# Reordering the stretch ahead of the loop in a modulated-attention and fusion-MLP kernel

## The chip, the cores and the metric

The kernel runs on one core of a Trainium2 chip. The metric is the device time of one execution in microseconds (us), median of the runs shown. The core's engines are TensorE (PE, matmuls), VectorE (DVE), ScalarE (ACT), GpSimd (POOL) and SyncE (SP, here only a queue of DMA issues). Each runs its own list of instructions strictly in order, and they meet only at semaphores.

## The reference

The input `x` is 4 x 1024 x 512, with conditioning vectors of 256, 64 and 32 numbers for each of the 4 batches. Two parts follow one another; both add their result to their input:

```
kx  = x @ (w * style * demod) + b              # modulated linear, weights differ by batch
A   = softmax(kx_heads @ kx_heads.T / sqrt(32)) # over the 16 heads of one token
x   = x + modulated_linear(A @ kx_heads)
h   = LN(LN(x, pw[id], pw_b[id]), cp[id], cp_b[id]);  t = LN(x, tm..);  s = LN(x, ms..)
m, n, r = x + LN(silu(cond @ W1 + b1) @ W2 + b2)     # for the three conditioning vectors
x   = x + LN(silu(concat(w0 h, w1 t, w2 m, w3 n, w4 r, w5 s) @ int_W1 + b) @ int_W2 + b)
```

The tables for gains and biases are small (5, 5 and 3 rows), so the kernel multiplies them by the parts of `int_W1` once, ahead of the loop, and adds the right row by a matmul with one-hot ids. The parts of `int_W1` for m, n and r act on the same `x`, so they are summed once into one weight (`x` below).

## The kernel before

The 4096 tokens are 32 tiles of 128. The loop runs k = 1 to 16. Pass k does the attention ("front") of tiles a = 2k and b = 2k+1 and the fusion MLP ("back") of tiles pa = 2k-2 and pb = 2k-1 side by side. Fp32 accuracy is got from products of a high and a low part (`three` on TensorE), so every operand and every weight is split: ACT rounds the high part, DVE or POOL subtracts for the low one.

Ahead of the loop stands a long straight stretch, about 88 us, in which the weights are loaded, modulated and split, the tables are made, and tiles 0, 1 and 2 go through parts of the attention. Its order is written out by hand on each engine. There is no planner. The names that matter:

- TensorE: `tables_tsh` multiplies the bias tables of t, s and h by `raw_t`, `raw_s`, `raw_h` (12 matmuls of 512 columns, three at a time on separate 32-column parts of the array). `tables_mnr` does the same with the rows of m, n, r, which ACT writes to `L` (L1013) from the transposed vectors of `vec_T`. `scores(g)` and `values(g)` are the two attention products of tile g in the PSUM tile `att`; `out_proj(g)` and `proj(g)` are the two modulated linears; `a_T`, `z_T`, `x_T`, `u_T` are transposes. `mlp1` and `mlp2` are the conditioning MLPs.
- ScalarE: `q_hi(g)` (L816) rounds the result of `proj(g)`; `e_first(g)` (L856) rounds the transposed softmax of tile g into `e`, `gain_tables` makes `Gt`, `Gs`, `Gh`, `split_hi` rounds a weight, `z_make` (L878) applies the first layer norm, `value_low` (L846) copies half of `values`.
- VectorE: `e_T` (L1329 to L1335) is the softmax's sum, division and transpose; `e_second` (L1339) the low part of `e`, on which `values` waits. `vectors_norm` and `vectors_end` (L1251, L1256, L1258) finish the m, n, r vectors in `p_h`, on which `vec_T` waits. `x_one` (L1358 to L1364) adds the residual and takes statistics; `q_lo` (L1290), `q_T` (L1297); `a_sum` (L1345, L1347); `x_weights` (L1284) sums the m, n, r weights into `stg_e`, 8 pieces in all; `x_low` (L1274) makes the low part of that sum, 4 pieces; `x1_lo(g)` (L1376) is the low part of the tile's x, which also frees the PSUM bank that `x_T(1)` waits for.
- GpSimd: no order changes there. It scales the scores, roots the variances, gathers pathway rows by DMA, and makes low parts of the weights t, s, h.
- SyncE: `blocks_q(g)` and `blocks_v(g)` copy transposed tiles into the block-diagonal tile `BD`, 4 DMAs each; `blocks_q(1)` waits for the end of `values(0)`.

Of the kernel before, what the change touches and what calls it, by code (L numbers as in the profile page):

```python
# [75 lines left out]
def build(nc, A, out):  # L76
    ctx = ExitStack()
    with ctx:
        s = {n: ctx.enter_context(nc.semaphore("s_" + n)) for n in SEMS}
# [321 lines left out]
        def _(e):  # L401
# [74 lines left out]
            def vec_T():  # L476
                e.wait_ge(s["h2"], 6)
                o = bank(("vT", 0))
                for c in range(4):
                    i = e.transpose(o[:, c * 128:c * 128 + 128], h2[:, c * 128:c * 128 + 128], ident[:, :])  # L480
                i.then_inc(s["vTr"], 1)

            def tables_tsh():

                e.wait_ge(s["LB"], 3)
                for n in "tsh":
                    e.wait_ge(s["c_r" + n], 16)
                for kt in range(4):
                    for n, quarter in (("t", 0), ("s", 1), ("h", 3)):
                        i = mm(Pp[quad(quarter), :], L[n][:, kt, :], raw[n][:, kt, :], start=(kt == 0))  # L490
                        if kt == 3:
                            i.then_inc(s["Pm"], 1)
# [13 lines left out]
            def proj(g, kts=range(4)):  # L506

                o = tok[1 if g else 0]
                on_bias = g > 3 and g % 2 == 0
                if kts[0] == 0:  # L510
                    if g == 0:
                        e.wait_ge(s["c_one"], 48)
                        e.wait_ge(s["tq"], 1)
                    elif on_bias:
                        e.wait_ge(s["sd"], g // 2 - 1)
                    elif g == 2:
                        e.wait_ge(s["ql"], 2)
                    elif g > 3:
                        e.wait_ge(s["wc"], g // 2 - 1)
                    elif g == 3:  # L520
                        e.wait_ge(s["ql"], 3)
                    e.wait_ge(s["xlo"], g + 1)
                for kt in kts:
                    if g % 8 == 0:
                        e.wait_ge(s["mwl"], 8 * (g // 8) + kt + 1)
                    i = three(o[:, :], xhi[:, kt, :], xlo[:, kt, :], WL["k", "h"][:, kt, :], WL["k", "l"][:, kt, :], kt == 0 and not on_bias)
                if kts[-1] == 3:
                    if not on_bias:
                        i = mm(o[:, :], selT[:, :].to_broadcast([128, 128]), tab[:, :])
                    i.then_inc(s["A"], 1)  # L530

            def scores(g):
                if g:
                    e.wait_ge(s["AVs"], 2 * g)
                e.wait_ge(s["bq"], 64 * (g + 1))
                for j in range(16):
                    both = att[:, j * 64:j * 64 + 64].rearrange("p (m t) -> p m t", t=2)
                    q = q12[:, j // 2, :, j % 2, :]
                    mm(both, diag(j, 0), q, start=(j % 8 == 0))
                    i = mm(both[:, :, 0], diag(j, 1), q[:, :, 0])  # L540
                    if j % 8 == 7:
                        i.then_inc(s["S"], 1)

            def values(g):
                e.wait_ge(s["bv"], 64 * (g + 1))
                e.wait_ge(s["e2"], g + 1)
                for j in range(16):
                    c = slice(j * 32, j * 32 + 32)
                    both = att[:, j * 64:j * 64 + 64]
                    mm(both, diag(j, 0), e12[:, c, :].rearrange("p m t -> p (m t)"), start=(j % 8 == 0))  # L550
                    i = mm(both.rearrange("p (m t) -> p m t", t=2)[:, :, 0], diag(j, 1), e12[:, c, 0])
                    if j % 8 == 7:
                        i.then_inc(s["AV"], 1)
# [23 lines left out]
            def out_proj(g):  # L577
                o = att if g == NG - 1 else tok[0]
                if g == NG - 1:
                    e.wait_ge(s["AVs"], 2 * g + 2)  # L580
                elif g % 2 == 0 and g:
                    e.wait_ge(s["x1"], g)
                elif g > 2:
                    e.wait_ge(s["w"], g - 2)
                elif g == 1:
                    e.wait_ge(s["x1"], 1)
                else:
                    e.wait_ge(s["ql"], 1)
                e.wait_ge(s["alo"], g + 1)
                for kt in range(4):  # L590
                    if g % 8 == 0:
                        e.wait_ge(s["mwl"], 8 * (g // 8) + 4 + kt + 1)
                    i = three(o[:, 0:512], ahi[:, kt, :], alo[:, kt, :], WL["o", "h"][:, kt, :], WL["o", "l"][:, kt, :], kt == 0)
                i.then_inc(s["O"], 1)
# [63 lines left out]
            proj(1)  # L658
            mod_rows(1)
            mlp1()  # L660
            tables_tsh()
            values(0)
            demod_T()
            mlp2()
            a_T(0)
            scores(1)
            out_proj(0)
            proj(2)
            vec_T()
            tables_mnr()  # L670
            values(1)
            z_T(0)
            a_T(1)
            scores(2)
# [81 lines left out]
        def _(e):  # L756
# [54 lines left out]
            def q_hi(g):  # L811
                e.wait_ge(s["A"], g + 1)
                e.wait_ge(s["sc"], 2 * g + 2)
                if g:
                    e.wait_ge(s["qT"], g)
                e.activation(qt[:, :, 0], tok[1 if g else 0][:, :], ACT.Copy, scale=inverse(g)).then_inc(s["qh"], 1)  # L816
# [35 lines left out]
            def e_first(g):  # L852
                e.wait_ge(s["ET"], 2 * g + 2)
                if g:
                    e.wait_ge(s["AV"], 2 * g)
                e.copy(e12[:, :, 0], att[:, 512:1024]).then_inc(s["e1"], 1)  # L856
# [88 lines left out]
            def gain_tables():  # L945

                e.wait_ge(s["tq"], 1)
                for i, n in enumerate("tsh"):
                    e.activation(GT[n][:, :], tab[:, :], ACT.Copy, scale=cst[:, 5 + i:6 + i]).then_inc(s["G"], 1)

            def split_hi(dst, src, sem):
                for kt in range(4):
                    i = e.copy(dst[:, kt, :], src[:, kt, :])
                i.then_inc(sem, 1)
# [53 lines left out]
            x_scaled()  # L1008
            exponential(1)
            gain_tables()  # L1010
            e.wait_ge(s["vTr"], 1)
            for i, n in enumerate("mnr"):
                j = e.activation(L[n][:, :, 0:24].rearrange("p k (r c) -> p k r c", c=8)[:, :, :, 0:4],  # L1013
                                 four(xp[XP["vT", 0][0]])[:, :, 32 * i:32 * i + 4].unsqueeze(2).to_broadcast([128, 4, 3, 4]), ACT.Copy, scale=w7[:, 2 + i:3 + i])
                j.then_inc(s["LB"], 1)
            q_hi(2)
            e_first(1)
            e.wait_ge(s["m2"], 3)
            e.wait_ge(s["c_rt"], 16)
            split_hi(W1["t", "h"], raw["t"], s["wh"])  # L1020
            z_make(0)
            value_low(1)
            e.wait_ge(s["Pm"], 15)
# [122 lines left out]
        def _(e):  # L1146
# [100 lines left out]
            def vectors_norm():  # L1247
                r = slice(0, 96)
                mv = small[r, 72:74]
                e.wait_ge(s["lnB"], 2)  # L1250
                e.tensor_scalar(h2[r, :], h2[r, :], mv[:, 0:1], small[r, 75:76], ALU.subtract, ALU.mult).then_inc(s["h2"], 1)  # L1251

            def vectors_end():
                r = slice(0, 96)
                e.wait_ge(s["h2"], 4)
                e.tensor_tensor(h2[r, :], h2[r, :], rv[1][r, :], ALU.mult).then_inc(s["h2"], 1)  # L1256
                e.wait_ge(s["h2"], 5)
                e.tensor_tensor(h2[r, :], h2[r, :], rv[2][r, :], ALU.add).then_inc(s["h2"], 1)  # L1258
# [19 lines left out]
            def x_weights(n, kts):  # L1278

                src, land = ((stg["a"], "c_rn"), (raw["r"], "c_rr"))[n - 1]  # L1280
                e.wait_ge(s[land], 16)
                e.wait_ge(s["xc"], n)
                for kt in kts:
                    i = e.scalar_tensor_tensor(out=stg["e"][:, kt, :], in0=src[:, kt, :], scalar=w7[:, 2 + n:3 + n], in1=stg["e"][:, kt, :], op0=ALU.mult, op1=ALU.add)  # L1284
                    if n == 2 or kt == 3:
                        i.then_inc(s["xc"], 1)
# [50 lines left out]
            def e_second(g):  # L1337
                e.wait_ge(s["e1"], g + 1)
                e.tensor_tensor(e12[:, :, 1], att[:, 512:1024], e12[:, :, 0], ALU.subtract).then_inc(s["e2"], 1)  # L1339
# [123 lines left out]
            score_sum(1)  # L1463
            less_max(1)
            vectors_norm()
            vectors_end()
            x_weights(1, (0,))
            e_T(1)
            x_one(0)
            e_second(1)  # L1470
            q_lo(2)
            q_T(2)
            a_sum(1)
            x_weights(1, (1, 2))
            a_lo(1)
            x_weights(1, (3,))
            v_stats(0)
# [4 lines left out]
            score_sum(2)  # L1482
            x_low((0,))
            x_one(1)
            x_low((1,))
            x1_lo(0)
            x_low((2, 3))
            e.wait_ge(s["Pm"], 16)
            e.wait_ge(s["c_rp"], 32)
            e.tensor_tensor(rp[:, :], rp[:, :], Pp[:, :], ALU.add).then_inc(s["pa"], 1)  # L1490
# [433 lines left out]
```

## Time and profile before

| | us |
|---|---|
| median of three runs | 871.07 |
| lowest, highest | 868.79, 872.23 |
| span of the profiled execution, first to last instruction | 867.6 |
| PE busy | 836.8 (96%) |
| DVE, POOL, ACT busy | 646.7, 605.7, 487.6 |
| mean granted TensorE clock | 0.989 of full |

The profile has the span of the profiled execution and no further time of its own for it; the median of the runs lies 3.5 us above the span. Busy shares are means over all stages: PE is nearly always busy from 92 us on, and has its gaps ahead of that.

### The profile page before, as it was taken

Reading aid. Unit: us, or ns where it says so; the run is one execution under the profiler, and the core shown is the slowest. Engines: PE = TensorE matmul, PEld = TensorE weight load, DVE = VectorE, ACT = ScalarE, POOL = GpSimd, SP = SyncE. Lnnn points to the kernel's source line nnn. Section 1 sums busy time; section 2 is a strip of 40 time slices with the busy share of each in tenths; the row PEclk is TensorE's granted clock in tenths of the full one; section 3 lists DMA queues with packets and bytes.
Section 4 is the critical chain, followed back from the end, with each engine's and each line's share of the span. In section 5 each row is a group of like instructions: output and inputs, shape, how many; then the busy total and the mean of one; then the engine's idle time right before and its main releaser. Section 6 shows DMA issues by size and latency. Waiting matters only on the chain.

```text
span 867.6 us, 19685 instructions
## 1 busy us (share of the span) xinstructions
PE 836.8 (96%) x7456; PEld 731.9 (84%) x7474; DVE 646.7 (75%) x1067; ACT 487.6 (56%) x851; POOL 605.7 (70%) x766
## 2 busy tenths in 40 slices
PE   5996999999999999999999999999999999999997
PEld 5853888988889898888989898888988898898986
DVE  3589778778786867678797877679797767677652
ACT  3567555565656465465656556465647546464531
POOL 2367998778786767768776866668787775756472
PEclk9998999999999999999999999999999999999999
DMA  8972233424343333525243332424343342323110
GB/s 277 419 268 62 71 91 105 126 63 150 83 151 81 98 93 86 128 51 158 71 149 89 107 93 69 127 68 145 83 123 91 87 117 49 104 68 83 47 50 25
DMA packets 104365, 95.55 MB, mean 110 GB/s; under 512 B 72880, under 2 KB 78160, under 8 KB 102608
## 3 DMA queue, kind: packets, MB, share of 16 engines
q1 hardware_dynamic: 95056, 69.26, 27.7%
q0 software_dynamic: 4608, 16.78, 7.1%
q10 hardware_dynamic: 4608, 8.25, 2.8%
q8 instruction: 60, 0.98, 0.5%
q14 instruction: 33, 0.27, 0.1%
HBM read 69.60 MB, written 8.40 MB: 90 GB/s over the span
## 4 chain that ended last, share of the span: by engine, by line
PE 88%; DVE 5%; DMA 2%; POOL 2%; issue 1%; ACT 1%; ACTq 0%; another core or an unknown queue 0%; DVEq 0%; POOLq 0%
PE acc L405 43%; PE tok L405 28%; PE att L405 8%; PE xp L558 6%; PE xp L405 3%; DMA kb<-in_kb 1%; DVE stg_e L1284 1%; DMA pgb<-in_pw,pidx 1%; DVE raw_k L1170 0%; DVE W1xl L1274 0%; POOL op0l L1706 0%; DVE qt L1290 0%; POOL W2l L1710 0%; DVE q L1297 0%; DVE BD L1185 0%
## 5 line engine op out<-in xcount | busy, mean ns | idle before, releaser
L1706 POOL TENSOR_TENSOR op1l<-ytmp,op1h 128x512 fp32r<-128x512 f32 x64 | 89.8, 1403 | 20.1 <-ACT op1h L912 19.6
L1652 POOL TENSOR_TENSOR xlo<-xraw,xhi 128x512 fp32r<-128x512 f32 x31 | 40.5, 1306 | 68.0 <-ACT xhi L804 68.0
L405 PE MATMUL acc<-op0h,W1xh 128*128 128x256 f32 x256 | 75.8, 296 | 1.4 <-DVE op0l L1376 1.1
L405 PE MATMUL acc<-op1h,W1th 128*128 128x256 f32 x256 | 75.0, 293 | 0.0
L405 PE MATMUL acc<-op1h,W1hh 128*128 128x256 f32 x256 | 73.7, 288 | 0.0
L405 PE MATMUL acc<-op0h,W1sh 128*128 128x256 f32 x256 | 73.7, 288 | 0.0
L405 PE MATMUL acc<-op1h,W1tl 128*128 128x256 f32 x256 | 72.4, 283 | 0.0
L405 PE MATMUL acc<-op1l,W1hh 128*128 128x256 f32 x256 | 72.4, 283 | 0.0
L405 PE MATMUL acc<-op1l,W1th 128*128 128x256 f32 x256 | 72.4, 283 | 0.0
L405 PE MATMUL acc<-op0h,W1sl 128*128 128x256 f32 x256 | 72.4, 283 | 0.0
L405 PE MATMUL acc<-op1h,W1hl 128*128 128x256 f32 x256 | 72.4, 283 | 0.0
L405 PE MATMUL acc<-op0l,W1sh 128*128 128x256 f32 x256 | 72.4, 283 | 0.0
L405 PE MATMUL acc<-op0l,W1xh 128*128 128x256 f32 x256 | 72.3, 282 | 0.0
L405 PE MATMUL acc<-op0h,W1xl 128*128 128x256 f32 x256 | 72.3, 282 | 0.0
L912 ACT CAST op1h<-ytmp 128x512 fp32r<-128x512 f32 x64 | 39.6, 619 | 46.9 <-DVE ytmp L1390 44.8
L1691 POOL TENSOR_TENSOR pgb<-z,pgb 128x512 f32<-128x512 f32 x32 | 48.0, 1499 | 15.1 <-DMA pgb<-in_pw,pidx 14.1
L1670 POOL TENSOR_TENSOR SE<-SE,wT 128x512 f32<-128x512 f32 x32 | 34.1, 1066 | 33.9 <-DVE SE L1324 33.6
L1390 DVE TENSOR_TENSOR ytmp<-zT,xp 128x512 f32<-128x512 f32 x64 | 43.6, 682 | 17.9 <-ACT zT L892 12.9
L405 PE MATMUL tok<-Wkh,xhi 128*128 128x512 f32 x128 | 56.0, 438 | 0.2
L405 PE MATMUL tok<-W2h,op0h 128*128 128x512 f32 x128 | 52.8, 412 | 0.0
L405 PE MATMUL tok<-Wkl,xhi 128*128 128x512 f32 x128 | 51.4, 402 | 0.0
L405 PE MATMUL tok<-Wkh,xlo 128*128 128x512 f32 x128 | 51.3, 401 | 0.0
(269 smaller groups left out, 3005.2 us busy)
## 6 DMA issues: line engine op xcount, KB each, us to landing
xsq<-in_x SPq DMA_DIRECT2D x32, 256.0 KB, 3.1
xb<-in_x SPq DMA_DIRECT2D x32, 256.0 KB, 3.0
out<-xb SPq DMA_DIRECT2D x32, 256.0 KB, 2.4
BD<-q SPq DMA_DIRECT2D x124, 64.0 KB, 2.1
BD<-v SPq DMA_DIRECT2D x124, 64.0 KB
xraw<-in_xT SPq DMA_DIRECT2D x30, 256.0 KB, 3.0
ring<-in_k_wT ACTq DMA_DIRECT2D x6, 256.0 KB, 3.3
dmb<-dm_rows SPq DMA_DIRECT2D x6, 256.0 KB, 3.9
```

The source lines that it names most:

```text
L405: return e.matmul(o, a, b, start=start, stop=True, skip_group_check=True)
L558: i = e.transpose(o[:, c * 128:c * 128 + 128], src[:, c * 128:c * 128 + 128], ident[:, :])
L912: e.copy(op[slot]["h"][:, :, half(g)], four(ytmp[YT[n, g][0]])).then_inc(s[f"o{n}h"], 1)
L1284: i = e.scalar_tensor_tensor(out=stg["e"][:, kt, :], in0=src[:, kt, :], scalar=w7[:, 2 + n:3 + n], in1=stg["e"][:, kt, :], op0=ALU.mult, o ...
L1390: e.tensor_tensor(four(y), src, four(xp[XP[n, g][0]]), ALU.mult).then_inc(s["p" + n], 1)
L1652: e.tensor_tensor(xlo[:, :, :], (xraw1 if g == 1 else xraw)[:, :, :], xhi[:, :, :].bitcast(F32), ALU.subtract).then_inc(s["xlo"], 1)
L1670: e.tensor_tensor(c, c, wT[g % 2][:, :].unsqueeze(2).to_broadcast([128, 32, 16]), ALU.mult).then_inc(s["wS"], 1)
L1691: e.tensor_tensor(pg, z[:, :], pg, ALU.mult).then_inc(s["v"], 1)
L1706: e.tensor_tensor(op[slot]["l"][:, :, half(g)], four(ytmp[YT[n, g][0]]), op[slot]["h"][:, :, half(g)].bitcast(F32), ALU.subtract).then_inc ...
```

## The change

Only the order of calls changes, on three engines; no instruction is added or removed.

- TensorE: `tables_tsh` moves from ahead of `values(0)` to behind `scores(1)`; `values(1)` moves from behind `tables_mnr` to ahead of `vec_T`.
- ScalarE: the three copies into `L` for m, n, r, with their wait for `vec_T`, move behind `q_hi(2)`, `e_first(1)` and the rounding of the t weights.
- VectorE: `e_T(1)` and `e_second(1)` move ahead of `vectors_end` and of `x_one(0)`; the first piece of `x_weights(1)` joins the second and third, behind `a_sum(1)`; `x1_lo(0)` moves ahead of the second piece of `x_low`.

```diff
 (TensorE)
             mlp1()
-            tables_tsh()
             values(0)
             demod_T()
             mlp2()
             a_T(0)
             scores(1)
+            tables_tsh()
             out_proj(0)
             proj(2)
+            values(1)
             vec_T()
             tables_mnr()
-            values(1)
             z_T(0)
 (ScalarE)
             exponential(1)
             gain_tables()
+            q_hi(2)
+            e_first(1)
+            e.wait_ge(s["m2"], 3)
+            e.wait_ge(s["c_rt"], 16)
+            split_hi(W1["t", "h"], raw["t"], s["wh"])
             e.wait_ge(s["vTr"], 1)
             for i, n in enumerate("mnr"):
...
-            q_hi(2)
-            e_first(1)
-            e.wait_ge(s["m2"], 3)
-            e.wait_ge(s["c_rt"], 16)
-            split_hi(W1["t", "h"], raw["t"], s["wh"])
             z_make(0)
 (VectorE)
             vectors_norm()
+            e_T(1)
+            e_second(1)
             vectors_end()
-            x_weights(1, (0,))
-            e_T(1)
             x_one(0)
-            e_second(1)
             q_lo(2)
             q_T(2)
             a_sum(1)
-            x_weights(1, (1, 2))
+            x_weights(1, (0, 1, 2))
...
             x_low((0,))
             x_one(1)
-            x_low((1,))
             x1_lo(0)
-            x_low((2, 3))
+            x_low((1, 2, 3))
```

## Rows read from the trace of the kernel before

**Rows 1.** The page: span, and busy time of each engine.
```profile
span 867.6 us, 19685 instructions
...
PE 836.8 (96%) x7456; PEld 731.9 (84%) x7474; DVE 646.7 (75%) x1067; ACT 487.6 (56%) x851; POOL 605.7 (70%) x766
```

**Rows 2.** PE's waits, 88 to 160 us: total, times, longest.
```profile
PE xp L558 <- DVE op0l L1376: 2.9, 1, 2.9
PE xp L558 <- ACT pgb L883: 1.3, 1, 1.3
```

**Rows 3.** Windows: length, each engine's busy time, clock, DMA share, GB/s.
```profile
90.00:120.00 30.00, 30.00 (x276) 27.21 (x276) 24.44 (x38) 17.29 (x32) 28.56 (x30) 0.99 0.36 85
```

**Rows 4.** Timeline of PE, 45 to 89 us: start, duration, operation, idle before.
```profile
45.80 0.62 PE L405 MATMUL acc<-raw_t,Lt 128*32 128x512 f32 x1
...
51.06 1.25 PE L405 MATMUL att<-e,BD 128*128 128x64 f16 x32
...
52.46 0.62 PE L405 MATMUL acc<-stg_b,p_hT 128*32 128x512 f32 x1
...
56.02 0.66 PE L558 MATMUL xp<-ident,ET 128*128 128x128 f32 x4
56.72 1.23 PE L405 MATMUL att<-q,BD 128*128 128x64 f16 x32
58.51 0.38 PE L405 MATMUL tok<-Woh,ahi 128*128 128x512 f16 x1 [0.55 <-issue]
...
60.90 0.58 PE L405 MATMUL tok<-Wkh,xhi 128*128 128x512 f32 x1
...
63.64 0.39 PE L405 MATMUL tok<-Wkh,xlo 128*128 128x512 f32 x1
...
88.04 1.09 PE L558 MATMUL xp<-ident,xb 128*128 128x128 f32 x4 [2.86 <-DVE op0l L1376]
```

**Rows 5.** Windows of 1 us; the clock is the third number from the end.
```profile
47.00:48.00 1.00, 1.00 (x9) 0.33 (x6) 1.00 (x2) 0.98 (x2) 0.00 (x0) 0.50 1.05 432
...
50.00:51.00 1.00, 1.00 (x9) 0.12 (x3) 1.00 (x2) 1.00 (x3) 0.63 (x1) 1.00 0.26 86
```

**Rows 6.** Timeline of DVE, 47 to 87 us.
```profile
47.75 0.73 DVE L1339 TENSOR_TENSOR e<-att,e 128x512 f16<-128x512 f32 x1
...
53.88 1.06 DVE L1347 STREAM_TRANSPOSE ET<-SE 128x512 f32<-128x512 f32 x1
...
61.50 1.43 DVE L1256 TENSOR_TENSOR p_h<-p_h,p_rv 96x512 f32<-96x512 f32 x1
62.96 1.67 DVE L1258 TENSOR_TENSOR p_h<-p_h,p_rv 96x512 f32<-96x512 f32 x1
64.55 0.74 DVE L1284 SCALAR_TENSOR_TENSOR stg_e<-stg_a,w,stg_e 128x512 f32<-128x512 f32 x1
...
66.94 0.73 DVE L1335 STREAM_TRANSPOSE att<-SE 128x512 f32<-128x512 f32 x1
...
71.71 0.76 DVE L1345 TENSOR_TENSOR SE<-att,SE 128x256 f32<-128x256 f32 x2
72.50 1.05 DVE L1347 STREAM_TRANSPOSE ET<-SE 128x512 f32<-128x512 f32 x1
73.47 2.87 DVE L1284 SCALAR_TENSOR_TENSOR stg_e<-stg_a,w,stg_e 128x512 f32<-128x512 f32 x2
...
85.91 1.39 DVE L1274 SCALAR_TENSOR_TENSOR W1xl<-stg_e,W1xh 128x512 fp32r<-128x512 f32 x1
```

**Rows 7.** Timeline of ACT, 62 to 72 us.
```profile
62.58 0.60 ACT L850 ACTIVATE att<-SE 128x512 f32<-128x512 f32 x1
...
65.94 0.86 ACT L816 ACTIVATE qt<-tok,tok_s 128x512 f16<-128x512 f32 x1
...
67.70 0.75 ACT L856 CAST e<-att 128x512 f16<-128x512 f32 x1 [0.90 <-DVE att L1335]
...
70.60 0.82 ACT L878 ACTIVATE z<-xb,nm,small 128x512 f32<-128x512 f32 x1
```

## The prediction

> **What bounds the kernel now.** I read the page first. PE is busy 836.8 of 867.6 us [rows 1], so a change of order can only move PE's 31 idle us, or change the clock that its matmuls get. Then I read PE's waits and the windows. Behind 88 us there are two waits worth a name up to 160 us, 2.9 us of `x_T(1)` on the low part of tile 0's x and 1.3 us of `u_T(2)` on ACT [rows 2], and 90 to 120 us is 30.00 busy of 30 [rows 3]. So the loop is bound by PE, and whatever the change does must show as a shift of the moment at which PE reaches those two places. The reader is to see in [rows 3] also that POOL is busy 28.56 of the same 30 us: POOL has hardly any room to catch up if it enters the loop late.
>
> Ahead of the loop I followed the chain of waits and then each engine's timeline. From scores(1) at 56.72 [rows 4] the chain leaves PE and runs almost wholly over DVE until the 2.9 us wait ends at 88.04 [rows 4]. In DVE's timeline the rows of that stretch stand nearly back to back, as the four from 61.50 on do [rows 6]. It is bound by DVE in its order, and PE's matmuls there lie beside it.
>
> **The change part by part.** I carry one number along: how much later (+) or earlier (-) each engine is than before.
>
> *values(0) without the tables ahead.* Before, tables_tsh ran from 45.80 to 51.06 and values(0) behind it [rows 4]. Its operand was ready at 48.48 [rows 6], so now it starts there, 2.6 us sooner, with PE idle between. demod_T and mlp2 follow at once. mlp2 took 3.56 us (52.46 to 56.02) [rows 4]. At full clock it would end near 53.6, but a_T(0) behind it needs the transpose that ends at 54.94 [rows 6]; that wait doesn't move, because it hangs on ACT's rounding of the o weights. So the gain for a_T(0) is at most 1.1 us. The clock decides what of it comes: before, at 47 us it was 0.50, the 1.2 GHz level, though PE was busy in the whole of that stretch, and 1.00 again at 50 us with the tables still running [rows 5]. Now there is a gap where those tables were, so I let half speed last into mlp2, until about 53 us. Then values(0) takes some 1.9 us instead of 1.25, and mlp2 ends at about 55.6. I take -0.4 us for a_T(0), scores(1) and the softmax chain behind them; the bounds are 0 and -1.1.
>
> The Trainium skill (TensorE: Matmul & The Clock Gate, Part 1) says that the throttled state is the default and that activity releases it. The trace agrees so far that the clock returned during the tables [rows 5]. By that rule the gap ahead of values(0) postpones the return, and the gain would be near -0.4 rather than the -1.1 of the full clock.
>
> *The tables behind scores(1).* scores(1) now ends near 57.55 (57.95 less 0.4). The tables are 12 matmuls of the same shape as mlp2's, so at full clock 3.5 us by mlp2 [rows 4] (at the mixed clock of before, 5.3). They cover 0.55 us that PE waited ahead of out_proj(0), and delay it by the rest. out_proj(0) took 2.39 us and proj(2) 3.13 (60.90 to the end of the row at 63.64) [rows 4]. So proj(2) ends at 57.55 + 3.5 + 2.4 + 3.1 = 66.55 instead of 64.03: +2.5 us. The bounds are 65.9 (early softmax) and 68.3 (5.3 us of tables).
>
> *Who is queued behind it.* On ACT, q_hi(2) waits for proj(2), and e_first(1) stands behind q_hi(2) in both orders. Before, q_hi(2) ran at 65.94 and cost nobody anything, since e_first(1) waited until 67.66 for DVE's transpose [rows 6, 7]. Now DVE does e_T(1) straight behind vectors_norm. The exponential, which ended at 63.18 [rows 7], ends near 62.75, and e_T(1) takes 2.4 us (as before: from the end of the row at 64.55 to 67.67, the end of the one at 66.94 [rows 6]), so the transpose is ready at 65.2. But ACT stands at q_hi(2) until 66.55. Its rounding and e_first(1), 0.8 and 0.75 us [rows 7], end at 68.1. e_second(1), next on DVE, waits from 65.2 to 68.1. That is 2.9 us of idle DVE with vectors_end, x_one(0), q_lo(2), q_T(2) and everything after it queued behind. There is another 1.7 us idle ahead of e_T(1) (from 61.1, where vectors_norm now ends, to 62.75), where vectors_end ran before.
>
> *vectors_end.* Its two additions took 1.43 and 1.67 us [rows 6], with POOL busy all the while. A comparable DVE instruction beside an idle POOL took 0.74 [rows 6]. At 68.7 us POOL is waiting for x_one(0), so I give both together 1.4 us instead of 3.1. This is the one thing the new order makes cheaper on DVE.
>
> *DVE's sum.* e_second, x_one, q_lo and q_T took the 4.05 us from 67.67 to 71.71 [rows 6]. Now they and vectors_end take 5.45, from 68.1: 73.6, that is +1.9. a_sum(1) is later still, because ACT reaches value_low(1) only behind z_make(0), which started 3.0 us after x_one(0) did (67.6 to 70.60) [rows 6, 7]. x_one(0) now starts at 70.1, z at 73.1, and half a copy later a_sum(1) starts at about 74.2: +2.5. Ahead of a_lo(1) stands one more piece of x_weights. Alone it took 0.74 us; two of them beside POOL took 2.87 [rows 6]. I take 1.2, between 0.7 and 1.4, nearer the latter since POOL does tile 0's affine and the low part of x(3) then. So DVE is +3.7 us from there on, through x_weights(2), x_one(1) and x_low. POOL follows (its root of tile 0 waits for DVE's v_stats, and the low parts of the t weights stand behind it): +3.6.
>
> *x_low.* Taking x1_lo(0) ahead of one piece of x_low saves 1.39 us [rows 6] for x_T(1), not for DVE as a whole. So x_T(1) is +3.7 - 1.4 = +2.3, and with it proj(3) and the first W1 matmuls. The weights' low part and the last sum ahead of them are also due 2.2 to 2.3 us after where W1 started, so they don't hold it longer.
>
> *tables_mnr.* It ran in a gap at 65.8. Now it waits for vectors_end (70.1), vec_T and ACT's copies, and runs from about 71 to 74, with z_T(0) due at 73.9 behind it: hidden. If it ran longer, a_T(1) at 76.1 is the next with work of weight, so up to 2 us more are covered. The same holds for values(1), at 68.8 instead of 70.0, and for the DMAs of blocks_q(1), which go out 2 us sooner; scores(1) waits for a_T(0) anyway.
>
> *In the loop.* PE arrives +2.3, DVE and POOL +3.6. PE's next wait is u_T(2), 1.3 us in [rows 2], at the end of a chain over POOL's gather of tile 2 and the affine behind it. POOL has only 1.4 idle us in the 30 up to 120 us [rows 3], and what it waited for there comes later now too. So it stays about +3.3 us there and PE's wait grows by 1. Behind that PE has nothing to win back. The sum is +3.3 us: 870.9 on the profiled span of 867.6. The median of the runs is 3.5 above the span, so 871.1 + 3.3 = 874.4.
>
> The Trainium skill (SBUF — State Buffer, SBUF: two separate sides) says that DVE instructions with two SBUF inputs and GpSimd instructions lock one shared pair of ports against each other, one waiting for the whole of the other. The trace agrees: 2.87 us for two of such pieces beside POOL against 0.74 for one alone [rows 6]. By the rule the moved x_weights piece would cost a whole POOL instruction more and DVE would be +3.9.
>
> **The rivals.**
> 1. *DVE's chain isn't held (the other side of the sign).* Place: e_second(1). If proj(2) ended by 64.4, ACT would be through in time and the 2.9 us of idle go. With the earliest start (-0.7 more) and the cheap x_weights piece (-0.5) the sum is 3.3 - 2.9 - 0.7 - 0.5 = -0.8: 870.3. For it speaks that this is where vectors_end gets cheaper; against it that out_proj and proj alone need 5.5 us and the tables 3.5. Even so it is not 0.5% faster; that would need the clock to stay high at 88 us as well. Chance 0.08, with 0.04 for faster by over 0.5%.
> 2. *It does nothing that the time shows.* Idle DVE is filled back by shorter waits on POOL, and the later wait of u_T doesn't grow: 3.3 less 1.0 (u_T) less 1.3 of port waits gives about +1: 872.1. Chance 0.19. For it: port waits are some 3.7 us of DVE's stretch by [rows 6] alone (3.1 for 1.4, 2.9 for 1.5, 1.4 for 0.7) and shift freely.
> 3. *The clock.* Place: tables_tsh, out_proj(0), proj(2). If the low level of [rows 5] comes with them, the tables take up to 7 us and what follows up to 3 more, all ahead of q_hi(2). It decides as soon as proj(2) ends behind 68.5; each us there is a us of DVE's idle. Two to three us more give +6: 877. Against it: by the trace the clock was full from 50 us on. Chance 0.16.
> 4. The forecast, +1.5 to +5, has 0.57.
>
> **How the numbers follow.** A measurement of this kernel tells about 0.5% (4.35 us) from no change, so the bounds are 866.7 and 875.4. Of the forecast's 0.57 some three quarters lie within; with rivals 1 and 2 that makes 0.66 for same. Slower gets the last quarter and nearly all of the clock rival: 0.30. Faster: 0.04. The range, 870.3 to 878.0, goes from rival 1's time to a little above rival 3's.
>
> **What would show it.** Right: PE idle ahead of values(0) for about 2.7 us; out_proj(0) starting near 61; a DVE wait of 2 to 3 us on ACT's e ahead of L1339; L1256 and L1258 near 0.7 us each; x_T(1) at about 90.3; the wait of u_T(2) over 2 us. Wrong: no DVE wait ahead of L1339, or x_T(1) ahead of 88; a clock of 0.5 between 57 and 66 us; or POOL catching up by 120 us.

## The result, and the profile after

The changed kernel took 873.97 us (median of 8 runs, 872.34 to 874.92) against 870.03 us (median of 8, 868.79 to 872.23) for the kernel before. The ratio is 1.0043, with a 95% interval of 1.0031 to 1.0055: slower by 3.9 us by the medians and 3.7 by the ratio, where 3.3 were forecast. The loss is clear of zero, and its middle value lies below the half per cent that was called no change.

The page of the changed kernel, span and busy times:

```profile
span 872.7 us, 19702 instructions
...
PE 840.6 (96%) x7474; PEld 733.7 (84%) x7474; DVE 644.6 (74%) x1067; ACT 488.0 (56%) x851; POOL 604.9 (69%) x766
```

The span is 5.1 us longer than in [rows 1], but not all of that is the change's. Here is DVE's timeline of the changed kernel, from e_second(0) on, the point at which the orders of the two kernels part:

```profile
49.23 0.72 DVE L1339 TENSOR_TENSOR e<-att,e 128x512 f16<-128x512 f32 x1
...
61.78 0.53 DVE L1251 TENSOR_SCALAR p_h<-p_h,small 96x512 f32<-96x512 f32 x1
64.07 0.69 DVE L1329 TENSOR_REDUCE small<-att 128x16 f32<-128x512 f32 x1 [1.75 <-ACT att L850]
...
69.50 0.73 DVE L1339 TENSOR_TENSOR e<-att,e 128x512 f16<-128x512 f32 x1 [2.96 <-ACT e L856]
70.12 0.67 DVE L1256 TENSOR_TENSOR p_h<-p_h,p_rv 96x512 f32<-96x512 f32 x1
70.83 0.69 DVE L1258 TENSOR_TENSOR p_h<-p_h,p_rv 96x512 f32<-96x512 f32 x1
...
75.61 0.76 DVE L1345 TENSOR_TENSOR SE<-att,SE 128x256 f32<-128x256 f32 x2 [0.69 <-ACT SE L846]
...
77.39 3.55 DVE L1284 SCALAR_TENSOR_TENSOR stg_e<-stg_a,w,stg_e 128x512 f32<-128x512 f32 x3
...
81.47 1.84 DVE L1284 SCALAR_TENSOR_TENSOR stg_e<-stg_a,w,stg_e 128x512 f32<-128x512 f32 x1
```

e_second(0) starts at 49.23, where it was 47.75 [rows 6]. Nothing ahead of it was changed. In this execution DVE waited 1.36 us instead of 0.45 for the load of `pidx` near 19 us, and the lag grew to 1.48 by here. So I take 1.48 us off the changed kernel's times before comparing, and give places as times since the start of e_second(0). By that the span grew by 3.6 us, close to the 3.9 of the medians. The reader is to see the two new waits, 1.75 us ahead of the softmax's sum and 2.96 us ahead of `e`, and vectors_end at 0.67 and 0.69 us instead of 1.43 and 1.67 [rows 6].

The second of these waits is for ACT, and ACT itself waited for PE. In ACT's timeline `q_hi(2)` (L816) is held by `proj(2)`, and `e_first(1)` (L856) comes only behind it:

```profile
68.07 0.83 ACT L816 ACTIVATE qt<-tok,tok_s 128x512 f16<-128x512 f32 x1 [2.17 <-PE tok L405]
68.76 0.71 ACT L856 CAST e<-att 128x512 f16<-128x512 f32 x1
```

PE's timeline of the changed kernel, with the places that [rows 4] has:

```profile
50.10 1.87 PE L405 MATMUL att<-e,BD 128*128 128x64 f16 x32 [2.73 <-DVE e L1339]
...
52.33 1.06 PE L405 MATMUL acc<-stg_b,p_hT 128*32 128x512 f32 x1
...
57.09 0.66 PE L558 MATMUL xp<-ident,ET 128*128 128x128 f32 x4
57.59 1.22 PE L405 MATMUL att<-q,BD 128*128 128x64 f16 x32
58.73 0.62 PE L405 MATMUL acc<-raw_t,Lt 128*32 128x512 f32 x1
...
62.30 0.39 PE L405 MATMUL tok<-Woh,ahi 128*128 128x512 f16 x1
...
92.22 0.98 PE L558 MATMUL xp<-ident,xb 128*128 128x128 f32 x4 [2.82 <-DVE op0l L1376]
...
96.40 0.47 PE L405 MATMUL acc<-op0h,W1xh 128*128 128x256 f32 x1
```

The gap ahead of values(0) is 2.73 us. values(0) takes 1.87 us and mlp2's first matmuls 1.06 instead of 0.62. The windows show the clock (third number from the end) at the 1.2 GHz level there, and at full speed only behind 54.8 us:

```profile
51.00:52.00 1.00, 1.00 (x21) 0.90 (x18) 1.00 (x3) 1.00 (x3) 0.00 (x0) 0.50 0.22 68
...
54.00:55.00 1.00, 1.00 (x9) 0.31 (x6) 0.97 (x3) 1.00 (x4) 1.00 (x2) 0.60 0.50 108
```

PE's waits from 88 to 160 us in the changed kernel are the two of [rows 2], hardly changed:

```profile
PE xp L558 <- DVE op0l L1376: 2.8, 1, 2.8
PE xp L558 <- ACT pgb L883: 1.4, 1, 1.4
```

So the loss isn't a longer wait at these two places. PE and DVE come to x_T(1) later together.

### The profile page after: what moved, and what is told of

It is laid out like the page before. It is cut to its first block, busy times and chain, and to the rows that moved or that the text cites. A ratio compares the mean times of both kernels' runs of the same rounds, so it can differ in the third digit from the quotient of the medians.

```text
span 872.7 us, 19702 instructions
## 1 busy us (share of the span) xinstructions
PE 840.6 (96%) x7474; PEld 733.7 (84%) x7474; DVE 644.6 (74%) x1067; ACT 488.0 (56%) x851; POOL 604.9 (69%) x766
## 4 chain that ended last, share of the span: by engine, by line
PE 86%; POOL 4%; DVE 3%; DMA 2%; issue 1%; ACT 1%; ACTq 0%; SPq 0%; POOLq 0%; DVEq 0%
PE acc L405 42%; PE tok L405 28%; PE att L405 8%; PE xp L558 6%; PE xp L405 3%; DMA kb<-in_kb 2%; DMA pgb<-in_pw,pidx 1%; POOL W1tl L1708 1%; POOL W1sl L1708 1%; DVE stg_e L1284 0%; POOL small L1596 0%; ACT BD L934 0%; SPq L303 0%; POOL pgb L1691 0%; POOL pgb L1689 0%
```

## The experiments

Each experiment was timed against the kernel before on the same chip, 5 to 12 runs each. The places below are us since the start of e_second(0), each from that kernel's profiled execution: the start of a_T(0); DVE's wait ahead of e_second(1); the starts of x_T(1), of the first W1 matmul, and of u_T(2). Behind u_T(2) the code of all kernels is the same, and this last stretch still took between 738.4 and 740.9 us. So the ratio is the verdict, and the places, each from a single execution, tell where it comes from; the two agree within about 1.7 us. W1 stands for the first W1 matmul.

| kernel | a_T(0) | wait | x_T(1) | W1 | u_T(2) | ratio to before |
|---|---|---|---|---|---|---|
| before | 8.27 | 0 | 40.29 | 44.16 | 81.28 | 1 |
| changed | 7.86 | 2.96 | 42.99 | 47.17 | 84.30 | 1.0043 [1.0031, 1.0055] |
| e1 tables home | 8.40 | 0.79 | 41.54 | 46.36 | 84.00 | 1.0019 [1.0007, 1.0031] |
| e2 e_first ahead | 8.07 | 0.80 | 41.01 | 44.15 | 82.52 | 1.0017 [1.0008, 1.0025] |
| e3 vectors early | 8.03 | 1.67 | 41.81 | 46.63 | 83.43 | 1.0021 [1.0009, 1.0033] |
| e4 x_low old | 8.21 | 2.96 | 44.63 | 49.44 | 87.11 | 1.0048 [1.0033, 1.0062] |
| e5 x_low only | 8.18 | 0 | 39.34 | 42.34 | 80.12 | 0.9994 [0.9982, 1.0006] |
| e6 tables only | 7.84 | 0.49 | 40.62 | 43.21 | 80.81 | 1.0009 [0.9998, 1.0020] |
| e7 tables behind proj | 8.16 | 0.81 | 41.08 | 44.23 | 82.62 | 1.0023 [1.0013, 1.0033] |
| e8 fill, clock | 7.88 | 2.96 | 42.99 | 46.17 | 84.00 | 1.0041 [1.0028, 1.0055] |
| e9 piece in gap | 8.33 | 0.80 | 39.73 | 42.86 | 81.61 | 0.9994 [0.9984, 1.0004] |
| e10 split tables, x_low | 7.15 | 0 | 37.65 | 40.79 | 78.83 | 0.9972 [0.9961, 0.9983] |
| e11 split tables | 7.49 | 0 | 39.31 | 43.14 | 80.14 | 0.9990 [0.9980, 1.0000] |
| e12 split and fill | 7.40 | 0 | 39.77 | 42.34 | 79.80 | 0.9978 [0.9969, 0.9987] |

**e1: the tables home again.** On TensorE, in the changed kernel:

```diff
             mlp1()
+            tables_tsh()
             values(0)
...
             scores(1)
-            tables_tsh()
             out_proj(0)
```

> The changed kernel with tables_tsh put back ahead of values(0); all else as changed. Forecast's theory (DVE is held by ACT's wait for proj(2) behind the tables): no gap ahead of values(0), proj(2) ends 2.5 us sooner than in the changed kernel, measured from e_second(0), the DVE wait ahead of e_second(1) falls from 2.96 us to below 0.8, and the time comes to +0.6 to +1.5 us over the kernel before (about 871.3; ratio 1.001 to 1.002). Rival (DVE's own new order, above all the x_weights piece, makes the loss): the wait falls, but the time stays within 1 us of the changed kernel's 873.97.

Measured 872.63 us, 1.0019 to before: 1.7 us over it by the ratio and 1.9 by the medians, a little more than the 0.6 to 1.5 that I expected. The wait fell to 0.79 us as forecast, and the time fell with it, by 0.0024 of the 0.0043. The rival, that DVE's own order makes the loss, has the rest of it: 0.0019 is left with the tables where they were. x_T(1) came 1.45 us sooner than in the changed kernel, W1 only 0.81. Between the two the granted clock was lower: 0.50 in e1 (89.34 to 94.16 us) against 0.59 in the changed kernel (92.22 to 96.40). At u_T(2) only 0.30 us were left in e1's profiled execution, less than its time gained.

**e2: e_first(1) ahead of q_hi(2).** On ACT, the tables left where the change put them:

```diff
-            q_hi(2)
             e_first(1)
+            q_hi(2)
```

> The changed kernel with e_first(1) ahead of q_hi(2) on ACT, so that nothing on ACT's way to e_second(1) waits for proj(2); the tables stay behind scores(1). Forecast's theory: the DVE wait ahead of e_second(1) falls from 2.96 to about 0.8 us (ACT's own 0.75), everything behind it comes 2.1 us sooner, and the time is 1.7 to 2.2 us below the changed kernel (ratio to before 1.002, about 871.9). Rival (the tables cost through out_proj(0) and proj(2) themselves, as PE work in the way): less than 0.7 us below the changed kernel.

Measured 872.45 us, 1.0017. DVE's waits from 60 to 72 us in e2:

```profile
DVE small L1329 <- ACT att L850: 1.8, 1, 1.8
DVE e L1339 <- ACT e L856: 0.8, 1, 0.8
```

Two lines exchanged on ACT give as much as the tables' return. So what this part of the loss hangs on isn't the tables' 3.5 us on PE, but that ACT stands at q_hi(2) with e_first(1) behind it. x_T(1) came 1.98 us sooner, as expected (2.1). W1 stands at 44.15, where it stood before the change, and yet the kernel is 1.5 us slower than before: u_T(2) is 1.24 us later. Between W1 and u_T(2) PE now waits 0.49 us for DVE's `e` and 0.30 for POOL's low part, which it doesn't in the kernel before. This is the lag of DVE and POOL that the prediction placed in the loop.

**e3: vectors_end ahead of e_T(1).** On DVE:

```diff
             vectors_norm()
+            vectors_end()
             e_T(1)
             e_second(1)
-            vectors_end()
```

> The changed kernel with vectors_end put back ahead of e_T(1) on DVE, in the 1.75 us in which DVE waits for the exponential. The two additions should take about 3 us again beside POOL (0.67 and 0.69 in the changed kernel), e_T(1) starts about 1.4 us later, and that is hidden behind the wait for q_hi(2), which shrinks to about 1.5 us; x_one(0) comes 1.3 us sooner and tables_mnr leaves the stretch behind values(1). Forecast's theory: 1.0 to 1.4 us below the changed kernel (about 872.7, ratio to before 1.003). Rival (a DVE idle time that is only refilled by slower instructions): no gain, within 0.4 us of the changed kernel.

Measured 873.07 us, 1.0021: below the changed kernel by about 1.9 us by the ratios and 0.9 by the medians, where 1.0 to 1.4 were expected (the intervals of the ratios just overlap). x_T(1) came 1.18 us sooner, u_T(2) 0.87. The timeline of e3:

```profile
62.07 1.43 DVE L1256 TENSOR_TENSOR p_h<-p_h,p_rv 96x512 f32<-96x512 f32 x1
63.53 1.64 DVE L1258 TENSOR_TENSOR p_h<-p_h,p_rv 96x512 f32<-96x512 f32 x1
65.10 0.68 DVE L1329 TENSOR_REDUCE small<-att 128x16 f32<-128x512 f32 x1
...
69.22 0.73 DVE L1339 TENSOR_TENSOR e<-att,e 128x512 f16<-128x512 f32 x1 [1.67 <-ACT e L856]
```

The same two instructions, a multiplication and an addition, take 3.07 us beside POOL and 1.36 without it. Dear as they are there, most of it lies in time that was lost anyway: the wait ahead of e_second(1) is 1.67 us instead of 2.96.

**e4: x_low in its old order.**

```diff
             x_one(1)
+            x_low((1,))
             x1_lo(0)
-            x_low((1, 2, 3))
+            x_low((2, 3))
```

> The changed kernel with x_low in its old order (second piece ahead of x1_lo(0)). If PE's entry into the loop sets the end (as the trace of the changed kernel has it: PE and POOL both 4.5 us later at values(2)), x_T(1) comes 0.7 to 1.4 us later and the time is 0.7 to 1.4 us above the changed kernel (about 875.1, ratio to before 1.006). Rival (POOL's and DVE's lag set the end through u_T(2), as the prediction had it): x_T(1) is later, but u_T(2) waits that much less, and the time is within 0.4 us of the changed kernel.

Measured 875.57 us, 1.0048. Against the changed kernel that is 0.4 us by the ratios and 1.6 by the medians, with intervals that overlap, so the time alone decides between neither theory. The places speak against the rival: x_T(1) is 1.64 us later, W1 2.27 and u_T(2) 2.81, and PE's wait at u_T(2) is no shorter (1.37 us against 1.39). By the places the reorder of x_low is the part of the change that helps. The times of e4, e5 and of e10 against e11 all point the same way, each by less than its intervals can tell.

**e5: the kernel before with that reorder alone.**

```diff
-            x_low((1,))
             x1_lo(0)
-            x_low((2, 3))
+            x_low((1, 2, 3))
```

> The kernel before with one part of the change alone: x1_lo(0) ahead of the second piece of x_low. Forecast's theory: x_T(1) comes 1.4 us sooner; W1 starts up to 1.4 us sooner, since the last sum and x1_lo(1) on DVE end 1.4 us ahead of where W1 started; behind it DVE and POOL have gained nothing, so part of it is given back at u_T(2). Time 0.3 to 1.4 us below before (ratio 0.9985 to 0.9997). Rival (POOL's chain to u_T(2) decides alone): W1 starts sooner, but the time is within 0.3 us of before.

Measured 869.82 us, 0.9994: 0.5 us or 1.0 below before by ratio and median, and not told from it. x_T(1) came 0.95 us sooner, not 1.4, since DVE now waited 0.38 us for ACT ahead of x1_lo(0). W1 came 1.82 us sooner: the clock from x_T(1) to W1 was 1.00 instead of 0.64, and the stretch took 3.00 us instead of 3.87. At u_T(2) 1.16 us were left.

**e6: the kernel before with the tables moved alone.**

```diff
             mlp1()
-            tables_tsh()
             values(0)
...
             scores(1)
+            tables_tsh()
             out_proj(0)
```

> The kernel before with one part alone: tables_tsh behind scores(1); the orders of ACT and DVE and of values(1) as before. Forecast's theory: the same delay of proj(2) (2.1 to 2.5 us), but now x_one(0) stands ahead of e_second(1) on DVE and hides a part; ACT's vec_T wait, q_hi(2) and e_first(1) come later, the DVE wait ahead of e_second(1) is about 1 us, a_sum(1) about 1.5 us later. Time 1.0 to 1.8 us above before (ratio 1.0012 to 1.002). Rival (the new DVE order alone makes the loss): within 0.5 us of before.

Measured 871.27 us, 1.0009 (0.9998 to 1.0020), below the 1.0012 that I expected at least; the interval holds it, and no loss as well. DVE in e6:

```profile
68.32 0.18 DVE L1364 BATCH_NORM_AGGREGATE small<-small 128x2 f32<-128x6 f32 x1
68.99 0.77 DVE L1339 TENSOR_TENSOR e<-att,e 128x512 f16<-128x512 f32 x1 [0.49 <-ACT e L856]
...
71.99 0.76 DVE L1345 TENSOR_TENSOR SE<-att,SE 128x256 f32<-128x256 f32 x2 [0.36 <-ACT SE L846]
```

The wait is 0.49 us, since x_one(0) still stands ahead of e_second(1). a_sum(1) is 0.33 us later than before, not 1.5. So the move of the tables alone costs at most 1.7 us and perhaps nothing; with DVE's new order it costs the 2.96 us wait. By the ratios the tables alone cost 0.8 us (e6), the new orders without them 1.7 (e1), both together 3.7. That the whole is more than the parts is shown by the waits (0.49, 0.79 and 2.96 us), and only suggested by the times.

**e7: the tables behind proj(2).** In the changed kernel:

```diff
             scores(1)
-            tables_tsh()
             out_proj(0)
             proj(2)
+            tables_tsh()
             values(1)
```

> The changed kernel with tables_tsh behind proj(2) instead of ahead of out_proj(0): the same matmuls, on TensorE between scores(1) and values(1) in both. Forecast's theory (what counts is that they stand ahead of proj(2), on which ACT waits): the DVE wait ahead of e_second(1) falls from 2.96 to about 0.8 us, the time to that of the kernel with e_first(1) ahead, 1.5 to 2.2 us below the changed kernel (ratio to before about 1.002). Rival (the gap and the low clock ahead of mlp2 cost, wherever the tables go): within 0.7 us of the changed kernel.

Measured 872.20 us, 1.0023, and the places are those of e2 within 0.1 us. That shows it from the other side: the same matmuls between scores(1) and values(1), with the same gap ahead of values(0), cost some 1.7 us less once proj(2) doesn't wait for them.

**e8: the clock at x_T(1).** In the changed kernel 12 matmuls into a free bank, whose result nobody reads, are added ahead of `x_T(1)`:

```diff
+                if k == 1:
+                    for _ in range(12):
+                        mm(mlp[:, :], xhi[:, 0, :], WL["k", "h"][:, 0, :], True)
                 if front:
                     x_T(pb)
```

> The changed kernel plus 12 matmuls of 128x512 into a free PSUM bank, whose result nobody reads, between the first quarter of proj(3) and x_T(1), where PE waits 2.8 us and the granted clock falls to 0.5. Clock theory: they last about 2.8 us in the wait, the clock stays at 1.0, and x_T(1) to the first W1 matmul takes 3.1 to 3.3 us instead of 4.18, so the time falls by 0.7 to 1.0 us (ratio to before about 1.0033). Rival (what the clock gives back is only waited for later, on DVE's x1_lo(1) and in the loop): W1 starts sooner, the time stays within 0.3 us. If the 12 run at 1.2 GHz they take 5 us and x_T(1) is up to 2 us later: slower.

Measured 873.59 us, 1.0041. PE in e8:

```profile
87.93 2.91 PE L405 MATMUL acc<-Wkh,xhi 128*128 128x512 f32 x12
90.90 0.63 PE L558 MATMUL xp<-ident,xb 128*128 128x128 f32 x4
...
94.08 0.36 PE L405 MATMUL acc<-op0h,W1xh 128*128 128x256 f32 x1 [0.25 <-DVE op0l L1379]
```

The clock stayed at 1.00, and x_T(1) to W1 took 3.18 us instead of 4.18. Of the 1.00 us that this gave, 0.30 were left at u_T(2), and 0.2 us in the time by the ratios. PE waited 0.25 us for DVE ahead of W1, 0.47 ahead of values(2), and 0.3 for POOL, none of which it did in the changed kernel. The rival fits: at this place most of what a faster PE gains is waited for later. The time alone, with intervals of 1.2 us to either side, doesn't separate the two theories; the places do.

**e9: the x_weights piece in the gap.** e2, and on DVE:

```diff
             vectors_norm()
+            x_weights(1, (0,))
             e_T(1)
...
             a_sum(1)
-            x_weights(1, (0, 1, 2))
+            x_weights(1, (1, 2))
```

> The changed kernel with e_first(1) ahead of q_hi(2), and the first piece of x_weights(1) taken back behind vectors_norm, into the 1.75 us in which DVE waits for the exponential. Forecast's theory (the moved piece costs DVE 1.2 us or more where the change put it, POOL being busy there): a_lo(1) and x_low come 0.7 to 1.2 us sooner than with e_first(1) ahead alone, and the time is 0.5 to 1.0 us below that kernel's (ratio to before 1.0006 to 1.0012). Rival: the piece is free where it is, time as there (ratio 1.0017).

Measured 870.31 us, 0.9994: 2.0 us below e2 by the ratios, where 0.5 to 1.0 were expected. DVE in e9:

```profile
62.29 1.55 DVE L1284 SCALAR_TENSOR_TENSOR stg_e<-stg_a,w,stg_e 128x512 f32<-128x512 f32 x1
64.12 0.69 DVE L1329 TENSOR_REDUCE small<-att 128x16 f32<-128x512 f32 x1 [0.29 <-ACT att L850]
...
75.28 2.90 DVE L1284 SCALAR_TENSOR_TENSOR stg_e<-stg_a,w,stg_e 128x512 f32<-128x512 f32 x2
...
78.70 0.74 DVE L1284 SCALAR_TENSOR_TENSOR stg_e<-stg_a,w,stg_e 128x512 f32<-128x512 f32 x1
```

Behind a_sum(1) the four pieces of the changed kernel took 3.55 + 1.84 us; three take 2.90 + 0.74. The piece thus cost 1.75 us where the change put it, and 1.28 us of it reached x_T(1) (e9 against e2). Only 0.65 of the 1.75 is the piece itself. The other 1.10 is the last piece, which overlaps POOL's addition on tile 2 in both orders. Here is that addition in the changed kernel and in e9:

```profile
81.49 1.27 POOL L1675 TENSOR_TENSOR xb<-xb,ob 128x512 f32<-128x512 f32 x1
```

```profile
79.04 1.53 POOL L1676 TENSOR_TENSOR xb<-xb,ob 128x512 f32<-128x512 f32 x1
```

In e9 DVE's piece is 0.34 us ahead, takes 0.74, and POOL's addition takes 1.53. In the changed kernel the two start together (81.47 and 81.49), POOL's takes 1.27, and DVE's piece takes 1.84. So it was DVE that waited there, and in the old order POOL. The same pair stands in every run: 1.83 to 1.84 us for DVE's last piece with the moved piece ahead of it (e1 to e4, e7, e8), 0.73 to 0.74 without (before, e5, e6, e9 to e12).

e9 has all of the change but two things, the place of this piece and the order of e_first(1) and q_hi(2), and its time isn't told from the kernel before (0.9984 to 1.0004). The parts that no run tested alone, values(1) ahead of vec_T and ACT's copies behind e_first(1), thus add no loss that the time shows.

**e10 to e12: a version that fills the gaps.** The experiments say: keep x_low's new order, keep proj(2) early, and don't leave PE idle ahead of values(0). In the kernel before, `tables_tsh` takes its `kt` range as an argument and is cut in three:

```diff
-            tables_tsh()
+            tables_tsh((0, 1))
             values(0)
             demod_T()
             mlp2()
+            tables_tsh((2,))
             a_T(0)
             scores(1)
+            tables_tsh((3,))
             out_proj(0)
```

e10 has this and the diff of e5; e11 has this alone; e12 is e10 with the matmuls of e8.

> The kernel before with x1_lo(0) ahead of the second x_low piece, and tables_tsh in three parts: half of it ahead of values(0), which fills PE's 2.7 us gap there, a quarter behind mlp2, while PE waits for the transpose of tile 0, a quarter behind scores(1), where PE waited 0.55 us. Theory: a_T(0) and the DVE chain behind it come 0.7 to 1.1 us sooner than before, PE has no gap in which the clock falls further, proj(2) is not later; the time is 1 to 2 us below before (ratio 0.998 to 0.999). Rival (low clock in mlp2 makes it end as late as in the changed kernel): a_T(0) only 0.4 us sooner, ratio 0.999 to 1.0.

> The same three parts of tables_tsh in the kernel before, with its own order of x_low. Theory: a_T(0) 0.7 to 1.1 us sooner, x_T(1) and W1 as much sooner, and here DVE and POOL gain as much as PE, so that nothing is given back in the loop: 0.7 to 1.1 us below before (ratio about 0.999). Rival: the gain is lost on ACT's value_low or POOL, ratio 1.0.

> The kernel with the tables in three parts and x1_lo(0) first, plus the 12 unread matmuls ahead of x_T(1) against the low clock. Theory: W1 starts up to 0.8 us sooner than without them where the clock was low, and DVE's and POOL's lag takes that back in the loop: within 0.4 us of the same kernel without them. Rival (clock): 0.5 to 1 us below it.

e10 took 868.13 us (7 runs, 867.41 to 869.23), 0.9972 of before (0.9961 to 0.9983): faster than both kernels, by 2.4 us than before and by some 6 than the changed one. PE in e10:

```profile
48.36 1.06 PE L405 MATMUL acc<-raw_t,Lt 128*32 128x512 f32 x1
...
49.38 1.62 PE L405 MATMUL att<-e,BD 128*128 128x64 f16 x32
50.84 0.38 PE L455 MATMUL xp<-ident,dmT 128*16 128x128 f32 x2
51.15 0.62 PE L405 MATMUL acc<-stg_b,p_hT 128*32 128x512 f32 x1
...
55.56 0.66 PE L558 MATMUL xp<-ident,ET 128*128 128x128 f32 x4
...
58.20 0.39 PE L405 MATMUL tok<-Woh,ahi 128*128 128x512 f16 x1
```

No wait stands between mlp1 and out_proj(0), mlp2 begins at full speed, and a_T(0) starts at 7.15, 1.1 us sooner than before, which is the bound that the prediction read from the transpose's end. u_T(2) came 2.45 us sooner, the same as the time. That is more than the 1 to 2 us expected. e11, without x_low's order, gave 869.55 us and 0.9990, as expected. e12 took 868.45 us and 0.9978, not told from e10. It is no test of the clock: in e10 the clock from x_T(1) to W1 is 1.00 already, and the wait that the 12 matmuls fill is only 0.86 us, so they held x_T(1) up by 2.12 us and W1 by 1.55, where I had expected W1 sooner.

## Why the prediction was right

It forecast 874.4 with +3.3 us; the move was +3.9, to 873.97. The level fits in part by luck: the forecast stood on 871.1 for the kernel before, whose median in the comparison was 870.03, and that 1.1 us too much made up for a move 0.6 too small. The mechanism, an ACT instruction held by proj(2) with DVE's next operand queued behind it, is what the trace and the runs show. Step by step, in us since e_second(0), after less before:

- *values(0), mlp2, a_T(0).* Forecast -0.4, measured -0.41. The clock did what was assumed: low through the gap and into mlp2, until 53.3 us in the kernel before's time, where 53 was assumed. How near the figure came is partly luck: with the same code up to there a_T(0) starts between 7.84 and 8.33 in the eight kernels that have the gap, and at 8.18 to 8.40 in the three with the tables at home (before, e1, e5). That the gap was the cause of mlp2's slow start is supported by e10, where the gap is filled and mlp2 starts with 0.62 us matmuls.
- *The wait on ACT.* Forecast 2.9 us, measured 2.96; proj(2) ended 2.29 us later than before, where 2.5 were forecast. The forecast's mechanism is shown by e2 and e7, which bring the wait down to 0.8 us in two different ways and win 2.3 and 1.7 us by the ratios. The idle time ahead of e_T(1) was forecast as 1.7 and is 1.75.
- *vectors_end.* Forecast 1.4 us, measured 1.36, and 3.07 again in e3, where it runs beside POOL. (Its two instructions are a multiplication and an addition, not two additions; their times don't hang on it.)
- *a_sum(1).* Forecast +2.5, measured +2.42 (75.61 - 1.48 - 71.71).
- *The x_weights piece.* This term was mis-sized: 1.2 us with bounds of 0.7 and 1.4, measured 1.75, since the last piece now loses the turn to POOL (1.84 us instead of 0.74). By the rule of the Trainium skill that the prediction quoted (SBUF — State Buffer, SBUF: two separate sides) the price was a whole POOL instruction more. The prediction worked that out as +3.9 for DVE, but 0.74 and the 1.27 of POOL's addition make 2.0 us and +4.5; right behind the pieces +4.22 was measured. The rule's 2.0 still comes nearer to 1.75 than my 1.2.
- *x_low and x_T(1).* Forecast +2.3, measured +2.70. DVE was +4.03 at x_one(1) instead of +3.7, and x_low's order took 1.32 off it instead of 1.4.
- *The loop.* This step failed as it stood: PE's wait at u_T(2) was to grow by 1 us, because POOL would be 3.6 late and PE 2.3. It stayed at 1.4. PE came into W1 as late as the others, +3.01: 0.4 from the piece and 0.3 from the low clock between x_T(1) and W1 (4.18 us against 3.87), which I had not counted. From there to u_T(2) the two kernels take the same, 37.13 and 37.12 us. The lag itself is real, and shows where PE is early: this stretch is 38.37 us in e2, 38.39 in e7 and 38.75 in e9, with the waits on DVE and POOL that e2 has.
- *The sum* at u_T(2) is +3.02 in the profile beside 3.3. That it came so near is luck too: the wait that didn't grow (1.0 too much) and PE's later arrival (0.7 too little) are errors of opposite sign. The 0.6 us behind it up to the end are within what the same code varies between executions.

The rival "DVE's chain isn't held" was worked out at -0.8 us for proj(2) in time, earliest start and cheap piece. Without the last two that is +0.4, and e2, which is this case, gives +1.5 by the ratio. So the wait was about half of the loss, 1.7 to 2.3 us of 3.7 by e7 and e2, and the moved x_weights piece was most of the rest (e9). Of the rival "it does nothing that the time shows" one half came, the wait of u_T(2) that doesn't grow. The rival with the clock, a low level in tables_tsh and out_proj(0), did not come: both ran at 1.00.

What stays open: by the time alone, e5 and e6 aren't told from the kernel before, and whether e4 is slower than the changed kernel isn't settled. What values(1)'s new place and ACT's moved copies do alone wasn't run.

## What to carry to other kernels

Before moving work on one engine, look for what stands queued behind the wait that it delays on another: here q_hi(2) starts 18.84 us after e_second(0) in the changed kernel and 19.06 in e2, and only where e_first(1) stands behind it does DVE wait 2.96 us. A block of matmuls that can fill a gap was worth most here cut to the gaps' sizes, ahead of nothing that others wait for (e10, e11). And where three engines enter a loop close together, making one of them earlier turns part of the gain into waiting (e8 kept 0.30 of 1.00 us, e5 1.16 of 1.82); in e10 the whole chain moved, and the 2.45 us at u_T(2) came out in the time.

## What the runs showed of the hardware

- One DVE multiplication or addition with two SBUF operands (L1256, L1258) took 0.66 to 0.69 us with GpSimd idle (the changed kernel, e1, e2, e4, e7 to e9) and 1.43 to 1.67 beside GpSimd's scaling and addition (before, e3, e5, e6, e10 to e12). GpSimd's addition there took 1.71 to 1.74 us in the same runs, and 1.26 to 1.29 in the others, but for e9, where an x_weights piece ran beside it instead (1.71).
- Where one such DVE instruction and one of GpSimd's overlap, who is first decides who is held: 0.74 and 1.53 us with DVE 0.34 us ahead (e9), 1.84 and 1.27 with both starting together (the changed kernel). A piece added on DVE ahead of them turned the one into the other and cost 1.10 us more than its own length.
- The granted clock between x_T(1) and W1 goes with how long PE had waited just before: 1.00 after 0.36 us (e5) and 1.66 us (e2), and after the fill matmuls (e8); 0.59 after 2.82 us (the changed kernel); 0.50 after 3.53 us (e1). The stretch took 2.59 us at 1.00 where PE waited for nothing in it (e6), 3.00 to 3.18 at 1.00 in e5, e2 and e8, where W1 came right behind DVE's x1_lo(1), 4.18 at 0.59 and 4.82 at 0.50. So a shorter chain on DVE that left PE waiting longer gave back 0.6 us of its gain in e1.
